# Scan inputs: half of the products of step size and u computed on GpSimd instead of VectorE

## The reference, cut to what matters

```python
xz = h @ W_in;  xm, z = split(xz, 2)
xm = silu(conv(xm))                                 # u in the kernel: 4 taps per channel
dtr, Bm, Cm = split(xm @ W_xp, [64, 80])
dt = softplus(dtr @ W_dt + b_dt)                    # the step size
def step(hst, inp):                                 # over the 1024 steps
    dt_t, B_t, C_t, x_t = inp
    hst = hst * exp(dt_t[:, :, None] * A) + (dt_t * x_t)[:, :, None] * B_t[:, None, :]
    return hst, einsum('bds,bs->bd', hst, C_t)
```

## Time and profile before

| | us |
|---|---|
| median of 3 runs | 6273.09 (6269.48 to 6273.27) |
| the profiled execution's own time | 6283.99 |
| its span in the profile | 6281.9 |
| PE busy in the span | 5507.6 (88%) |
| DVE busy | 4683.8 (75%) |
| ACT busy | 4204.6 (67%) |
| POOL busy | 2479.7 (39%) |
| line 1701 on DVE, both layers | 64 instructions |

### The profile page before, as it was taken

The page is one execution under the profiler, slowest core; times in us unless marked ns, Lnnn a source line. Parts: engine busy times, 40 slices in busy tenths (PEclk is TensorE's granted clock), DMA queues, the critical chain, the costliest instruction groups (busy, mean ns, idle before and its releaser), DMA issues. The chain is left out here.

```text
span 6281.9 us, 85971 instructions
## 1 busy us (share of the span) xinstructions
PE 5507.6 (88%) x30568; PEld 3521.0 (56%) x30568; DVE 4683.8 (75%) x5712; ACT 4204.6 (67%) x6218; POOL 2479.7 (39%) x1098
## 2 busy tenths in 40 slices
PE   8989999998899989996788888888999678888886
PEld 3446666664455534443666666653444466666664
DVE  3349999996555545555999999984554699999996
ACT  2238888884232235556989898973555699999994
POOL 0000000000000000002999999971000499999997
PEclk9999999999999999997999999998999899999999
DMA  6453343323311033335656566633443655656566
GB/s 235 181 143 78 82 88 82 85 52 132 116 44 51 27 119 148 147 137 178 163 155 163 155 164 155 165 86 108 150 150 136 198 146 156 156 154 160 156 157 209
DMA packets 571257, 842.72 MB, mean 134 GB/s; under 512 B 100672, under 2 KB 240064, under 8 KB 570832
## 3 DMA queue, kind: packets, MB, share of 16 engines
q1 hardware_dynamic: 559312, 811.92, 44.3%
q0 software_dynamic: 5120, 16.78, 0.8%
q10 hardware_dynamic: 6400, 8.52, 0.4%
HBM read 544.23 MB, written 292.81 MB: 133 GB/s over the span
## 5 line engine op out<-in xcount | busy, mean ns | idle before, releaser
L1982 POOL TENSOR_TENSOR scan_hC<-scan_h,scan_Crep 128x1024 f32<-128x1024 f32 x1024 | 2395.4, 2372 | 2396.9 <-DVE scan_h L2235 2363.6
L2161 ACT ACTIVATE scan_a<-scan_dt,scan_A 128x512 f32<-128x512 f32 x2048 | 1368.4, 697 | 89.2 <-DVE scan_h L2235 71.8
L2031 PE MATMUL scan_y<-ident,scan_hC 128*128 128x128 f32 x8192 | 1115.2, 280 | 301.4 <-POOL scan_hC L1982 296.1
L2031 PEld LDWEIGHTS scan_y<-ident,scan_hC 128*128 128x128 f32 x8192 | 906.5, 142 | 687.0 <-POOL scan_hC L1982 638.7
L2235 DVE TENSOR_TENSOR_SCAN scan_h<-scan_a,scan_carry,scan_h 128x512 f32<-128x512 f32 x1024 | 1216.9, 1260 | 22.2 <-ACT scan_a L2161 19.4
L2235 DVE TENSOR_TENSOR_SCAN scan_h<-scan_a,scan_h 128x512 f32<-128x512 f32 x1024 | 1155.7, 1200 | 60.9 <-ACT scan_a L2161 60.3
L2137 ACT COPY scan_h<-scan_drive 128x1024 f32<-128x1024 f32 x1024 | 1041.7, 1017 | 179.9 <-PE scan_drive L2019 166.7
L2019 PE MATMUL scan_drive<-scan_Bd,scan_dT 128*128 128x256 f32 x4096 | 751.7, 306 | 134.8 <-ACT scan_h L2137 78.6
L2019 PEld LDWEIGHTS scan_drive<-scan_Bd,scan_dT 128*128 128x128 f32 x4096 | 559.6, 193 | 187.7 <-issue 101.3
L861 DVE CUSTOM_DVE_ANT_0 att_sm<-att_S,att_mneg 128x1024 f32<-128x1024 f32 x512 | 621.8, 1215 | 16.0 <-POOL att_mneg L787 15.8
L919 ACT ACTIVATE att_pr<-att_sm,att_nmax 128x1024 f32<-128x1024 f32 x512 | 590.5, 1153 | 57.9 <-DVE att_nmax L861 45.0
(11 more groups left out here) (189 smaller groups left out, 6173.9 us busy)
## 6 DMA issues: line engine op xcount, KB each, us to landing
scan_dT<-scratch_dtuT SPq DMA_DIRECT2D x512, 256.0 KB, 6.4
scratch_dtuT<-ssmin_dT SPq DMA_DIRECT2D x128, 512.0 KB, 3.3
scan_Crep<-scratch_bc SPq DMA_DIRECT2D x64, 1024.0 KB, 9.5
att_q<-scratch_q_split SPq DMA_DIRECT2D x256, 128.0 KB, 4.5
att_k<-scratch_k_split SPq DMA_DIRECT2D x256, 128.0 KB, 4.7
scratch_uD<-ssmin_uD SPq DMA_DIRECT2D x64, 512.0 KB, 3.4
scratch_z<-ssmin_zt SPq DMA_DIRECT2D x128, 256.0 KB, 2.3
scratch_dt<-ssmin_dt SPq DMA_DIRECT2D x64, 512.0 KB, 2.6
```

The lines of the kernel that those rows point to most:

```text
L1982: nc.gpsimd.tensor_tensor(hC[k % 2][:], of, Crep[:, 2 * p:2 * p + 2, :], ALU.mult).then_inc(s["scaled"].handle, 1)
L2031: last = nc.tensor.matmul(y[j][:, t, :], hC[k % 2][:, i, t * P:(t + 1) * P], ident[:], start=(p == 0 and i == 0 and t == 0), stop=False, i ...
L2161: nc.scalar.activation(a[(2 * k + i) % 3][:], dt[j][:], ACT.Exp, scale=A[:, m, 2 * p + i:2 * p + i + 1]).then_inc(s["decayed"].handle, 1)
```

## The change

The products of tiles 4 to 7 of each batch move from VectorE to GpSimd, 4 of 8 per batch, 32 of 64 in all, with a count of their own (`pool_step`, called `dtu_late`). `finish_dt` on DVE ends after the addition for m >= 4. PE's `turn` waits for the old count for m < 4 and for the new one for m >= 4. DVE's relu of tiles 0 to 3 of the next batch waits for the new count, since it writes the `dt` buffer that GpSimd reads. In layer 3, GpSimd's queue now holds the gathers of batches 0 and 1 first, and then, per batch, the gather of the batch after next followed by four products.

```diff
+        @block.gpsimd
+        def _(pool):
+            if gather is not None:
+                for it in range(2):
                     rows.gather_rows(pool, it)
+            for it in range(B):
+                if gather is not None and it + 2 < B:
+                    rows.gather_rows(pool, it + 2)
+                for m in range(4, IB):
+                    w(pool, "uD", it * IB + (m + 1))
+                    w(pool, "dt", it * IB + (m + 1))
+                    nc.gpsimd.tensor_tensor(u[:, m], dt[m % 4][:], u[:, m], ALU.mult).then_inc(dtu_late.handle, 1)
...
             def turn(it, m):
-                w(pe, "dtu", it * IB + (m + 1))
+                if m < 4:
+                    w(pe, "dtu", it * 4 + (m + 1))
+                else:
+                    pe.wait_ge(dtu_late.handle, dtu_late.at(it * 4 + (m - 3)))
...
                     dve.wait_ge(dt_out[m % 4].handle, dt_out[m % 4].at(it * 32 + (m // 4) * 16))
+                    if it and m < 4:
+                        dve.wait_ge(dtu_late.handle, dtu_late.at((it - 1) * 4 + (m + 1)))
...
                     nc.vector.tensor_tensor(dt[m % 4][:], dt[m % 4][:], ea[m % 4][:], ALU.add).then_inc(c["dt"].handle, 1)
+                    if m >= 4:
+                        return
                     w(dve, "dt", it * IB + (m + 1))
                     w(dve, "uD", it * IB + (m + 1))
                     nc.vector.tensor_tensor(u[:, m], dt[m % 4][:], u[:, m], ALU.mult).then_inc(c["dtu"].handle, 1)
...
+    core.pool_step.stage_added(4 * B)
```

More of the change, by code:

```diff
@@ L1339, in ssm_inputs @@
         dT_out = [core.stage_stored[0:2], [core.count(f"ssm_dT_out{th}") for th in range(2)]]
-        dt_out = core.stage_stored[6:10]
+        dt_out, dtu_late = core.stage_stored[6:10], core.pool_step
         Z_FIRST = 4
@@ L1443, in _ @@
             w(sp, "B_out", 256 * B)
-        if gather is not None:
-            @block.gpsimd
-            def _(pool):
-                for it in range(B):
+        @block.gpsimd
+        def _(pool):
+            if gather is not None:
+                for it in range(2):
                     rows.gather_rows(pool, it)
+            for it in range(B):
[5 more added lines that the diff above has]
+                    nc.gpsimd.tensor_tensor(u[:, m], dt[m % 4][:], u[:, m], ALU.mult).then_inc(dtu_late.handle, 1)
         @block.tensor
@@ L1751, in ssm_inputs @@
     for n, per in (("x_evac", 2 * IB), ("conv", IB), ("u", IB), ("proj", 1), ("proj_copy", 1), ("bc_out", 16), ("dtp", IB),
-                   ("z", IB), ("relu", IB), ("log", IB), ("dt", IB), ("dtu", IB), ("uD", IB), ("zt", 2 * TT), ("step", 3 * IB),
+                   ("z", IB), ("relu", IB), ("log", IB), ("dt", IB), ("dtu", 4), ("uD", IB), ("zt", 2 * TT), ("step", 3 * IB),
                    ("turned", 2 * IB), ("hi", 2 * IB), ("lo", 2 * IB), ("B_turned", 1), ("B_hi", 1), ("B_lo", 1),
```

## The result

| | before | after |
|---|---|---|
| median, us | 6275.69 (6259.44 to 6291.45, 20 runs) | 6282.81 (6277.23 to 6289.52, 20 runs) |
| the profiled execution's own time | 6283.99 | 6277.37 |
| its span | 6281.9 | 6274.9 |
| POOL busy in the span | 2479.7 | 2573.9 |

The ratio is 1.0014, with a 95% interval of 1.0008 to 1.0021: the change costs about 9 us (5 to 13) where 15 of gain were forecast. 6282.8 lies outside the range of 6253 to 6278.

A forecast was written before the change was run, and what follows sets the result against it. PE, busy 94% of both stages, bounds them, idling for DVE's `lo` at six places; 4.6 + 2.2 + 4.2 (load) + 2.6 (clock) + 1.2 (ends) = 14.8 us off 6273.1 gives 6258.3, range 6253 to 6278.

The forecast's parts named there:

- the first rival: GpSimd and DVE cannot read two SBUF tiles each at the same time; slower by about 20 us, 6293; chance 17%.
- Cost: none: Products added on GpSimd: hidden by the next batch's x phase, in time for tile 4, so costing nothing.
- What was removed: Four products per batch leave DVE's queue before `lo` of tile 2: 4.9 us less in front of it.
- The waits in layer 3: PE's idle time before turning tile 3 goes after batches 0 and 1: 2.3 us each, 4.6 in all.
- After batch 2: PE's wait for `lo` of tile 2 goes, without statistics there: 1.1 us in each layer, 2.2 in all.
- GpSimd's own price: One product on GpSimd takes 2.37 us, taken from the scan's multiplication of the same shape.
- The rival's own size: Exclusion of two-input SBUF reads: layer 3 and both batch 2 places lose about +20 us, 6293; chance 17%.
- The load: Layer 2 after batches 0 and 1: batch 2's rows or the like land 2.1 us earlier, 4.2 in all.
- The clock: Layer 2 after batches 0 and 1: shorter idle times keep the clock up at 65% each; 2.6 us for both.
- The stage's end: Last batch of each layer: `lo` and tile 5's store come earlier; 0.6 us twice, 1.2 in all.
- the low end: Stage's end: GpSimd late with its product, -0.5 us, against +1.1 at the high end.

The follow-up runs named there:

- e7: Kernel before with a stage of further DVE/GpSimd pairs measured by themselves ahead of it, among them scans with a PSUM input; span 6411.2 us.
- e5: Kernel before with a stage of DVE/GpSimd pairs measured by themselves ahead of it, among them additions beside products; span 6427.9 us.
- e4: Changed kernel with each GpSimd product replaced by a scalar operation that reads u alone; 6268.64 us, one run.
- e2: Kernel before without the products of tiles 4 to 7 on either engine; 6254.44 us, ratio 0.997.
- the first execution: Kernel before, unedited: the profiled execution that the prediction read; 6283.99 us.
- the others: Further executions of the kernel before's stages: run again unedited (6279.06 us), or with probe stages ahead of it (spans 6427.9 and 6411.2 us).
- e11: Kernel before run again, unedited, as a control of how far a stage repeats; 6279.06 us.

## Why the prediction was wrong

**The step that failed** is in the first rival: "in the scan DVE runs 18 scans, each with two SBUF inputs". They have one. `scan_a`, the first input, is a PSUM tile (line 1793: `a = [psum(f"a{k}", [P, HALF]) for k in range(3)]`). So the earlier trace rows show an operation with one SBUF input beside GpSimd, which runs undisturbed in e7 as well (17.94 and 17.94). They can't speak against an exclusion of operations that read two. The row was right and the reading of its names was not: the names tell the tile, not the memory it is in. Without that argument little stood against the rule of the Trainium skill (SBUF — State Buffer, Who interferes with whom), which names exactly this pair; e5 bears it out, 22.07 us for 9.17 and 13.82. The rule speaks of any GpSimd instruction that reads SBUF, and there the measurement is narrower: the single-input one of e4 left every addition at 1.226 us or less. The exclusion should have had most of the chance. Instead the prediction wrote "Cost: none" for the products on GpSimd, and that term is the one that came out wrong.

**What was removed: right in kind and nearly in size.** The waits in layer 3 were put at 2.3 each, and e2 gives 155.68 - 153.20 = 2.5. After batch 2 they were put at 1.1, and e2 gives 119.42 - 118.14 = 1.3. Without GpSimd's products the middle of the two stages is 11.2 us shorter (6.2 + 5.0) than in the first execution and 13.4 to 14.6 us shorter than in the others, where 13.6 was forecast. That the sum comes out so well is in part luck. In layer 2 after batches 0 and 1 the load and the clock were to give 6.8, and e2 gives 2.7 + 1.0: the clock fell both times. In layer 3 against the other executions each place gives 4.0 to 4.2 instead of 2.3, since the clock that was lost there too comes back; the prediction had no term for it. The whole of e2 is 0.3% faster.

**What was added: "Cost: none" was wrong.** GpSimd's own price was right (2.34 to 2.35 where nothing disturbs it), and tile 4 was in time in the middle of the stage. The price is on DVE: 20.3 us over both layers, by e2 against the changed kernel. Minus the 11.2, that leaves 9.1 by the first execution of the kernel before; by the others the gain is 13.4 to 14.6, which leaves 5.7 to 6.9.

**The rival's own size** was +20, and measured is +9 or less. In layer 3 after batches 0 and 1 it had `lo` 1.9 us later and 4.2 us lost each; `lo` was 1.56 later, and 4.3 and 2.9 were lost (160.01 and 158.53 against 155.68 and 155.67). After batch 2 it had 5.6 each; measured were 2.2 in layer 3, where the clock stayed up, and 3.6 in layer 2. In layer 2 after batches 0 and 1 it had 0, since the wait for the load hides the stretching; in fact 2.3 and 1.6 were gained, as the load also came earlier. It also left out the convolution's scalar operation, which reads one tensor and is stretched all the same (1.5 us of the 6.6). The mechanism was right, its list of operations one short, and its sum 10 us too high.

**The load.** Forecast 2.1 us earlier at each of two places; 1.5 at the landing, and 1.1 to 1.3 at PE. It was issued 2.35 us earlier, so 0.8 was lost between issue and landing, within the ends of 0 and 2.4.

**The clock.** I reckoned that an idle time under about 3.3 us keeps it and over 3.5 loses it. The changed kernel kept it after 3.15 us of idle time in layer 3 (next turning 7.86 us later) and lost it after 3.16 in layer 2 (9.28 us), and the kernel before lost it after 2.17 or 2.18 in four executions of five. The length of the idle time alone doesn't decide, so two rows of the scans were no ground for the term. One of the two was misread as well. The turning behind the 3.29 us took 1.22 us, which was taken for a clock that stayed up; the rows right behind it in the same trace say that it fell:

```profile
5605.70 1.20 PE L2019 MATMUL scan_drive<-scan_Bd,scan_dT 128*128 128x256 f32 x4
...
5607.55 1.79 PE L2031 MATMUL scan_y<-ident,scan_hC 128*128 128x128 f32 x8
```

```profile
5606.00:5610.00 4.00, 4.00 (x25) 4.00 (x24) 2.20 (x3) 2.32 (x4) 3.93 (x3) 0.61 0.10 27
```

The step ahead of the idle time had these matmuls in 0.71 and 1.09 us, and the granted clock from 5606 to 5610 averages 0.61. So the clock fell after both idle times of the earlier trace rows, and no row stood for keeping it at over 3 us.

What became of the term: after the two idle times of 4.09 us it fell both times, at the second only behind the turning (1.16 us, but the next 9.57 later). Before, the next came 10.46 and 9.94 later, now 9.24 and 9.57: 1.6 us of the 2.6.

**The stage's end.** Put at 1.2 us of gain; in layer 2, from the addition of tile 4 to the scan's first cast, it was 25.7 us before (2878.98 to 2904.70) and is 26.3 (2876.61 to 2902.93). GpSimd at 2.35 us per product is late, as the low end had it. Nor was there anything to gain: e2, with no products of tiles 4 to 7 at all, takes 25.7 us here in both layers. PE in the changed kernel:

```profile
2881.23 1.09 PE L1492 MATMUL ssmin_X<-ident,ssmin_u 128*128 128x128 f32 x8 [1.14 <-POOL ssmin_u L1456]
2883.54 1.97 PE L1492 MATMUL ssmin_X<-ident,ssmin_u 128*128 128x128 f32 x8 [1.23 <-POOL ssmin_u L1456]
2887.50 1.97 PE L1492 MATMUL ssmin_X<-ident,ssmin_u 128*128 128x128 f32 x8 [1.99 <-POOL ssmin_u L1456]
```

**What stays open.** What makes the scans scatter by up to 17 us wasn't looked into. Nor was it settled what besides idle time decides when the clock falls, why DVE's scalar operation with one tensor input is stretched, or why a single-input operation on GpSimd does so little. e4, e5 and all from e7 to e11 are one execution each, so what they say rests on their rows and stages and not on their times.

## What to carry to other kernels

Before an operation is given to GpSimd because it is idle, list what DVE runs at that time and in which memory each input lies: in these runs a GpSimd product of two SBUF tensors took turns with DVE's large operations on SBUF, so the work wasn't moved off DVE: where the two meet, each product takes 2.3 us of DVE's time and not the 1.2 that it saved. If a row is to show that two engines don't disturb each other, look up where its tiles were allocated. If a row is to show that the clock stayed up behind an idle time, read the rows after it too, and more than one execution. And before moving work to another engine, try moving it within its queue: putting the same products behind the instruction that someone waits for gave all of the gain, and then showed the next wait (the load), which was worth about as much again.

## What the runs showed that was not expected

- The exclusion is a strict alternation. Eight additions beside six products: six additions wait for a product each, two run free, 6 x 3.3 + 2 x 1.15 = 22.1 us (22.07 measured).
- DVE's scalar operation of 128x1024 (0.67 us each, eight in a row) with one tensor input is stretched too, eight beside six products from 5.39 to 17.92 us, and even by fills (9.94 us), which do nothing to additions.
- A one-input GpSimd operation (3.6 to 4.6 us) hardly disturbs additions (11.69 us for eight instead of 9.17; in the kernel not at all), and accumulations by at most 0.66 us in the kernel.
- The same program keeps the clock at two idle times of 2.18 us in one execution and loses it at the same places in four others, which moves its stage by about 2 us.
- Two stages of the same code, the scans, scatter by 13 to 17 us between executions while the stages beside them mostly repeat within a few tenths, and within 2.4 us in the case above.
